# A fused layernorm, attention and expert layer on one core: stack loads in six transfers of 16 rows, statistics in four pieces, normalization on ScalarE, and the zeroed rows and first maxima at other places

## What is computed

```python
def reference(L0_attn_x, L0_attn_w_qkv, L0_attn_w_out, L0_ffn_gate_w, L0_ffn_wg, L0_ffn_wu, L0_ffn_wd):
    x = L0_attn_x
    xn = _layernorm(x, axis=-1)
    s = _L0_attn_ref(xn, L0_attn_w_qkv, L0_attn_w_out)
    g = _silu(_L0_ffn_ref(xn, L0_ffn_gate_w, L0_ffn_wg, L0_ffn_wu, L0_ffn_wd))
    x = x + s * g
    return x
```

## Time and profile before

| what | value |
|---|---|
| device time, median of 3 runs | 1719.01 us (1713.76 to 1734.11) |
| device time of the profiled execution | 1720.51 us |
| its span, first to last instruction | 1718.8 us |
| mean granted clock of TensorE, share of full | 0.965 |
| PE, DVE, ACT, POOL busy, share of the span | 91%, 81%, 68%, 10% |

### The profile page before, as it was taken

How to read it: one execution, slowest core, us unless ns; L and a number is a source line. 1 busy time by engine, 2 the same in 40 slices (tenths; PEclk the granted TensorE clock), 3 DMA queues, 4 the chain that set the end, 5 groups by cost and what they waited for, 6 DMA issues and landing times.

```text
span 1718.8 us, 29455 instructions
## 1 busy us (share of the span) xinstructions
PE 1560.9 (91%) x9121; PEld 670.6 (39%) x9121; DVE 1385.8 (81%) x1541; ACT 1174.3 (68%) x2349; POOL 169.3 (10%) x174
## 2 busy tenths in 40 slices
PE   4869799996889999999999999999999999999998
PEld 2534333333543333333333333333333333333336
DVE  6657799994348899999999999999999999999805
ACT  1332148784557777778777778777778777778771
POOL 3542222210002220000001000000010000000100
PEclk8989779998989999999999999999999999999999
DMA  3354312322432221211111122111111211111203
GB/s 133 135 181 145 124 40 71 89 77 55 140 95 64 72 69 53 80 42 41 42 41 41 40 62 68 40 40 40 40 40 40 80 50 41 40 40 40 59 4 114
DMA packets 73595, 116.51 MB, mean 68 GB/s; under 512 B 25040, under 2 KB 60240, under 8 KB 66384
## 3 DMA queue, kind: packets, MB, share of 16 engines
q1 hardware_dynamic: 65408, 101.87, 18.9%
q0 software_dynamic: 3072, 8.39, 1.6%
q10 hardware_dynamic: 5072, 5.72, 1.0%
HBM read 75.31 MB, written 39.85 MB: 67 GB/s over the span
## 4 chain that ended last, share of the span: by engine, by line
PE 71%; ACT 16%; DMA 4%; DVE 4%; issue 3%; SPq 1%; POOL 0%; ACTq 0%; DVEq 0%
PE ps L1042 29%; PE ps L1053 29%; ACT arena L548 15%; PE ps L984 3%; PE ps L1033 2%; PE ps L985 1%; PE ps L1124 1%; PE ps L1139 1%; PE ps L1007 1%; DMA x_sb<-in_x 1%; PE ps L1105 1%; PE ps L1169 1%; DMA arena<-xs_d 1%; DMA arena<-arena 1%; DVE arena L644 1%
## 5 line engine op out<-in xcount | busy, mean ns | idle before, releaser
L663 DVE TENSOR_REDUCE arena<-ps 128x1 f32<-128x1024 f32 x1000 | 1182.6, 1218 | 124.1 <-PE ps L1033 114.9
L548 ACT ACTIVATE arena<-ps 128x512 f32<-128x512 f32 x2048 | 1059.7, 603 | 269.6 <-PE ps L1042 267.8
L1033 PE MATMUL ps<-ks,qs 48*128 48x512 f32 x2000 | 803.3, 475 | 5.7 <-DVE arena L663 4.3
L1042 PE MATMUL ps<-qs,ks 50*128 50x512 f32 x2048 | 751.9, 447 | 62.1 <-ACT arena L548 30.5
L1042 PEld LDWEIGHTS ps<-qs,ks 50*128 50x128 f32 x2048 | 340.6, 185 | 683.7 <-issue 433.0
L1053 PE MATMUL ps<-arena 128*32 128x512 f32 x4096 | 548.9, 608 | 0.8 <-ACT arena L548 0.8
L1033 PEld LDWEIGHTS ps<-ks,qs 48*128 48x128 f32 x2000 | 334.6, 187 | 54.6 <-DVE arena L663 22.4
L1053 PEld LDWEIGHTS ps<-arena 128*32 128x32 f32 x4096 | 80.7, 108 | 129.3 <-ACT arena L548 112.4
L918 POOL COPY arena<-v_sb 128x256 f32 (+1 forms) x32 | 13.3, 417 | 1077.8 <-ACT arena L540 1076.2
L478 ACT COPY arena<-ps 128x512 f32<-128x512 f32 x32 | 18.8, 586 | 86.3 <-PE ps L985 86.3
L984 PE MATMUL ps<-arena 128*128 128x512 f32 x128 | 76.5, 683 | 0.7 <-ACT arena L469 0.7
(11 more groups left out here) (101 smaller groups left out, 577.5 us busy)
## 6 DMA issues: line engine op xcount, KB each, us to landing
parts_d<-arena SPq DMA_DIRECT2D x64, 256.0 KB, 2.8
qs<-parts_d SPq DMA_DIRECT2D x64, 256.0 KB
ks<-parts_d SPq DMA_DIRECT2D x64, 256.0 KB
qs<-parts_d SPq DMA_DIRECT2D x64, 128.0 KB
ks<-parts_d SPq DMA_DIRECT2D x64, 128.0 KB
xs_d<-arena SPq DMA_DIRECT2D x13, 384.0 KB, 5.3
arena<-xs_d SPq DMA_DIRECT2D x13, 384.0 KB, 3.9
ys_d<-arena SPq DMA_DIRECT2D x13, 384.0 KB, 2.8
```

What stands on the lines that cost most here:

```text
L548: nc.scalar.activation(prob[kb % 2][:, c * W:(c + 1) * W], ps[:, bank, :], ACT.Exp, scale=SCALE).then_inc(exp_done[bank], 1)
L663: nc.vector.tensor_reduce(most[head_slot][:, tile, u:u + 1], ps[:, AB + 2 * u:AB + 2 + 2 * u, :], AX.XY, ALU.max).then_inc(a_reduced[u], 1)
L1033: ins = nc.tensor.matmul(ps[:, AB + c, :], qs[head_slot][ABASE:ABASE + KR, tile * P:(tile + 1) * P].bitcast(F32R), ks[head_slot][ABASE:ABA ...
L1042: nc.tensor.matmul(ps[:, bank, :], ks[s][0:KS, kb * P:(kb + 1) * P].bitcast(F32R), qs[s][0:KS, c * W:(c + 1) * W].bitcast(F32R), start=Tru ...
```

## The change

It has six parts.

1. `stack_loads` fills each stack with three transfers of 16 rows, in all six for the two stacks, with no broadcast. The bytes are the same. `LOADS` becomes 6.
2. The statistics are taken in four pieces (tiles 0 to 3, 4 to 7, 8 to 15, 16 to 31). DVE does the last piece inside the tile loop: two tiles of `bn_stats` behind each of the tiles 0 to 7, and the short steps behind tile 7. The wait for the weights ahead of the first statistics is gone. The buffers for statistics get a place of their own.
3. The groups 1 to 7 are normalized by ACT, tile by tile, as x times the inverse deviation plus a shift (`Identity` with scale and bias). Group 1 comes before the loop, and tile t + 8 at the end of step t. DVE makes the shift with one more short step per piece. POOL keeps the rotary additions alone.
4. ACT loads the table of the square root ahead of the first one, and the table of the exponential behind the last high part, with a dummy activation on one column.
5. SP zeroes two sets of 384 rows behind each of the first seven pairs of tiles, in place of one behind each of 13, and ahead of the stack loads.
6. The maxima of tiles 12 and 13 of head 0 are computed in the last two steps of the setup, between the turns of tiles 30 and 31, and no longer behind it.

```diff
-    LOADS = 4
+    LOADS = 6
...
         def stack_loads(eng, head, qstack, kstack, base, done):
 
             rows = bass.ds(head * DH, DH)
-            eng.dma_start(qstack[base:base + 2 * DH, :],
-                          parts_d[0, 0, rows, :].unsqueeze(0).to_broadcast([2, DH, L])).then_inc(done, 16)
-            eng.dma_start(qstack[base + 2 * DH:base + 3 * DH, :], parts_d[1, 0, rows, :]).then_inc(done, 16)
-            eng.dma_start(kstack[base:base + 2 * DH, :], parts_d[:, 1, rows, :]).then_inc(done, 16)
-            eng.dma_start(kstack[base + 2 * DH:base + 3 * DH, :], parts_d[0, 1, rows, :]).then_inc(done, 16)
+            for i, (q_part, k_part) in enumerate(((0, 0), (0, 1), (1, 0))):
+                at = base + i * DH
+                eng.dma_start(qstack[at:at + DH, :], parts_d[q_part, 0, rows, :]).then_inc(done, 16)
+                eng.dma_start(kstack[at:at + DH, :], parts_d[k_part, 1, rows, :]).then_inc(done, 16)
...
+                for i in range(2 * p, min(2 * p + 2, NF // ZR)):
+                    clear_rows(i)
                 if p == NT // 4 - 1:
...
-                if p < NF // ZR:
-                    clear_rows(p)
...
+            def normal(t):
+
+                if t % GT == 0:
+                    act.wait_ge(norm_ready, max(k for k in range(len(XCUT) - 1) if XCUT[k] <= t) + 1)
+                ins = nc.scalar.activation(gate[:, t, :], x_sb[:, t, :], ACT.Identity, bias=shift_x[:, t:t + 1],
+                                           scale=rstd[:, t:t + 1])
+                if t % GT == GT - 1:
+                    ins.then_inc(xn_ready, 1)
...
+            act.wait_ge(first_ones, 1)
+            nc.scalar.activation(table_in[32:64, 0:1], ks[0][32:64, 0:1], ACT.Sqrt, scale=0.0)
+            root(0)
...
-            act.wait_ge(var_ready, 2)
-            nc.scalar.activation(tmp[:, 3, GT:NT], tmp[:, 2, GT:NT], ACT.Sqrt).then_inc(std_ready, 1)
+            root(1)
+            for t in range(GT, 2 * GT):
+                normal(t)
+            root(2)
             for t in range(NT):
...
                     high_part(t - LAG)
+                if t + 2 * GT < NT:
+                    normal(t + 2 * GT)
+                if t == 2 * GT - 1:
+                    root(3)
             for t in range(NT - LAG, NT):
                 high_part(t)
+            nc.scalar.activation(table_in[32:64, 1:2], ks[0][32:64, 0:1], ACT.Exp, scale=0.0)
...
-            dve.wait_ge(first_loaded, 16 * 2)
-            moments(0, (0,))
...
-            moments(1, (1, 2, 3))
+            for k in range(2):
+                dve.wait_ge(x_loaded[k], 16)
+                statistics(XCUT[k], XCUT[k + 1])
+                moments(k)
+                inverse(k)
...
-            for t in range(NT - LAG, NT):
-                low_part(t)
+                if t < 2 * GT:
+                    statistics(XCUT[3] + 2 * t, XCUT[3] + 2 * t + 2)
+                if t == 2 * GT - 1:
+                    moments(3)
+                    inverse(3)
+                    assert count[0] == SETUP_STEPS
+            for t in range(NT, NT + LAG):
+                reduce_early(t - EARLY, 0)
+                low_part(t - LAG)
+                reduce_early(t - EARLY, 1)
...
-            normal(1)
-            normal(2)
             for t in range(NT):
                 add_turned(t)
-                n, j = divmod(t, GT)
-                if j == 2 and n + 3 < NG:
-                    normal(n + 3)
...
-            for t in range(NT - LAG, NT):
-                turn_q(t)
+            for t in range(NT, NT + LAG):
+                score_early(t - EARLY, 0)
+                turn_q(t - LAG)
+                score_early(t - EARLY, 1)
```

More of the change, by code:

```diff
@@ L201, in layer_kernel @@
         std_ready = sem("std_ready")
[L202 removed]
+        norm_ready = sem("norm_ready")
         xn_ready = sem("xn_ready")
@@ L581, in link, with statistics, moments @@
                     dve.wait_ge(dve_step, base[0] + count[0])
-            def moments(k, pieces):
-                ts = slice(XCUT[pieces[0]], XCUT[pieces[-1] + 1])
-                for i in pieces:
-                    dve.wait_ge(x_loaded[i], 16)
-                    for t in range(XCUT[i], XCUT[i + 1]):
-                        nc.vector.bn_stats(stats[:, t, :], x_sb[:, t, :]).then_inc(stats_done, 1)
+            def statistics(lo, hi):
+                for t in range(lo, hi):
+                    nc.vector.bn_stats(stats[:, t, :], x_sb[:, t, :]).then_inc(stats_done, 1)
+            def moments(k):
+                ts = slice(XCUT[k], XCUT[k + 1])
                 dve.wait_ge(stats_done, ts.stop)
@@ L605, in _ @@
                 nc.vector.memset(ks[i][32:64, :], -1.0).then_inc(first_ones, 1)
-            dve.wait_ge(first_loaded, 16 * 2)
-            moments(0, (0,))
-            for j in range(GT):
-                ins = nc.vector.tensor_scalar(gate[:, j, :], x_sb[:, j, :], mean[:, j:j + 1], rstd[:, j:j + 1],
-                                              ALU.subtract, ALU.mult)
-            ins.then_inc(xn_ready, 1)
-            moments(1, (1, 2, 3))
+            for k in range(2):
[3 more added lines that the diff above has]
+                inverse(k)
+                if k == 0:
+                    for j in range(GT):
+                        ins = nc.vector.tensor_scalar(gate[:, j, :], x_sb[:, j, :], mean[:, j:j + 1], rstd[:, j:j + 1],
+                                                      ALU.subtract, ALU.mult)
+                    ins.then_inc(xn_ready, 1)
+            dve.wait_ge(x_loaded[2], 16)
+            statistics(XCUT[2], XCUT[3])
+            moments(2)
+            inverse(2)
+            dve.wait_ge(x_loaded[3], 16)
             dve.wait_ge(weights_loaded, 16 * NW)
@@ L644, in reduce_early @@
                 nc.vector.tensor_reduce(most[0][:, t, u:u + 1], ps[:, 6:8, :], AX.XY, ALU.max).then_inc(a_reduced[u], 1)
-            assert count[0] == SETUP_STEPS
             for t in range(NT):
@@ L726, in _ @@
             choose()
-            for t in range(NT - EARLY, KB):
+            for t in range(NT + LAG - EARLY, KB):
                 for u in range(2):
@@ L1059, in _ @@
             pe.wait_ge(qkv_out, NT)
-            for t in range(NT - EARLY, AHEAD):
+            for t in range(NT + LAG - EARLY, AHEAD):
                 if t == KB:
```

25 lines of the change are left out of this document (11 added, 14 removed).

## The result

The changed kernel takes 1674.54 us (median of 4 runs, 1672.07 to 1677.56) against 1716.77 us before (4 runs). The ratio is 0.9757, with a 95% interval of 0.9726 to 0.9789: faster, by 42 us. The forecast was 1665.1. Some of the 48.5 is chance: it is 6 us more than the medians give.

What follows compares the result with a forecast made beforehand. PE was taken to bound the heads (134.97 of 140 us busy), so only its waits could be won: 17.3 + 11.5 + 10.6 + 10.7 + 1.6 + 2.4 + 1.3 = 55.4 off 1720.51 gave 1665.1 us, range 1652 to 1688.

Steps and rivals of the forecast that it cites:

- Start and tiles 5 to 20: Setup: PE's 9.69 us wait for group 1 goes, 17.3 us gained to tile 5; undisturbed groups then gain 11.5.
- The rival of a setup bound by its chain: Setup: late ACT copies hold DVE and PE's turns, 4.0 us a tile for 3.3, 14 us less gain, 1679; chance 0.15.
- The first stack load: PE's 13.10 us wait at the first early score: six 16-row transfers land by 118.3, gain 10.6, bounds 5 and 13.
- Two of the signs named for a right forecast: First early score near 89 us after a 2 to 3 us wait; sorted rows landing within 5 us of issue.
- Ports: Stack loads: 16 rows in 16 partitions run at half rate, 2 us more at each of two waited loads, 1669; chance 0.12.
- The experts: PE's 12.09 us wait at the experts' first sorted rows: they land at 404.5, gain 10.7, bounds 5 and 12.1.
- The reciprocal's wait: DVE's 1.59 us wait at 556 for a small transfer behind a stack load goes: 1.6, bounds 0 and 2.5.
- The slower rival: Heads: six transfers fill all engines ahead of the small transfer of sums; DVE waits in 31 heads, 49 us; chance 0.02.
- End of the setup: Two tiles of maxima leave the run behind the loop, 5.1 us; the loop ends 2.7 later; net 2.4, bounds 0 and 5.
- The table's term: First exponential: the exponential's table load of 1.28 us that stood ahead of it is hidden; gain 1.3 us.
- What the clock gives back after shorter waits is not counted: Whole kernel: any gain from PE's granted clock after shorter waits was left out of the sum of 55.4 us.
- forecast as summed: Device time of the whole kernel with the terms as added up, 1655 to 1676 us; chance 0.60.

Runs made afterwards that it cites:

- e4: Changed kernel with groups 1 to 7 normalized by POOL again, the four pieces of statistics kept: 1688.37 us.
- m1: Transfers of 8 KB rows alone on an idle core, x copied unchanged, each set twice; six of 16 rows as in the kernel took 8.5 us.
- e1: Changed kernel with the four old stack transfers put back: 1688.81 us.
- e5: Changed kernel with the zeroing of 384 rows back behind each of the first 13 pairs of tiles: 1669.33 us.
- e3: Changed kernel with the maxima of tiles 12 and 13 computed behind the setup loop again: 1672.87 us.
- e10: Changed kernel with each block's rows on every fourth partition in the maxima's stacks (free rows zeroed once by POOL), every third in the others: 1673.13 us.
- e6: Changed kernel without the two table loads ahead of their use: 1673.14 us.
- e9: Changed kernel with each block's rows on every third partition and the zeroing back behind each of 13 pairs of tiles: 1674.67 us.

## Why the prediction was right and where it failed

**Start and tiles 5 to 20** came out as worked: 17.3 and 11.5 forecast, 17.3 and 11.7 measured, tile 5 at 33.00 and groups at 13.30 us. The cause, POOL's pass over DVE's product, was there again in e4 (2.07 for 0.69). That the wait of 9.69 us was the late statistics' shows in e4 as well, where it stays away. Four normalizations on ACT took 2.08 us, 0.52 each, where 0.384 had been taken from another activation; with 2 us in hand it didn't matter. The rival of a setup bound by its chain did not come; its only trace is the wait of 0.88 us that had been charged with 1.5.

**The first stack load** is where the sum failed first. The step was "So the transfers of 16 rows (128 KB) take 0.35 us on all engines": the bursts of the earlier trace rows were each a transfer with none of its kind ahead of it. From "by 115.9, and the last lands 2.5 us later" came a load of 4.8 us, bound by its issues. It took 8.5, bound by 1.14 us for each queued transfer, and the term of 10.6 measured 7.2. It was inside its bounds of 5 to 13. Two of the signs named for a right forecast failed with it: the first early score came at 92.72 after a wait of 5.90, not near 89 after 2 to 3, and the sorted rows 6.9 us after their issue, not within 5. The rival named Ports had the mechanism; it had a chance of 0.12, because I took the burst in the earlier trace rows for a rate. Its price from those bursts, 2 us a load, was still too low: 3.6 us. That the old 32-row transfers were the slow ones, at one or two tenths busy, was right (12.7 us for two alone in m1, and the waits in e1).

**The experts.** The term of 10.7 measured 9.3: PE's wait fell from 12.09 to 3.96, which is 8.1, and the rest of the stretch gave 1.2. That rest isn't told from chance: with waits of 4.0, 4.1 and 3.9 us the stretch from the fourth to the fifth reciprocal took 131.3 us in the changed kernel, 132.6 in e5 and 134.0 in e3. The step that failed is the same, "behind 2 us of wide transfers". e10 takes the wait down to 1.8.

**The reciprocal's wait** of 1.59 us in one head went, and with what lay behind it 2.5 was won for 1.6. The slower rival, a wait at each head, has no row: in the heads between the experts and the last ones the DMA ends no wait of the reciprocal.

**End of the setup.** The term of 2.4 came at 1.8, but not by its mechanism, so this near hit is luck. The step that failed was "so the loop ends some 2.7 us later": the stretch grew by 4.4 us against before (16.00 for 11.55) and by 4.8 against e3, and of the 5.1 us that leave the run behind the loop 0.6 and 0.2 remain. The other part of the 1.8 is one step at half clock fewer than before (1.7 us), less 0.5 for the step behind the first early score. The table's term of 1.3 holds: without the dummy activation the way from head 0 to the first exponential is 1.3 us longer in e6 (2.19 for 0.91). Neither shows in the time. "What the clock gives back after shorter waits is not counted" left out a place where it takes: 3.0 us in the first head.

The terms that came short, 3.4, 1.4, 0.6 and 3.0, less 1.5 that came over, are the 6.9 us between 55.4 and 48.5. By the medians 42 us were won; the execution profiled before was 3.7 us above its median, and the one after 2.2 below. The time fell into the stretch of "forecast as summed", 1655 to 1676, near its slow end. The price of the rival Ports, 1669, lies in the same stretch and nearer, so the time alone doesn't tell which of the two rates held; the rows do.

## What to carry to other kernels

Take the rate of a queued transfer from a row that has several of them in a queue: one burst shows what a lone transfer does (2.7 us, nearly all latency) and hides a limit that nearly doubled the load. Where the rows of an operand may stand in any order, spread those of one transfer over the partitions: every fourth in place of adjacent ones took six transfers from 8.4 to 5.8 us, and PE's wait in the kernel from 5.9 to 3.2. Look where the free rows are zeroed: on POOL at the start it cost DVE and PE 2.3 us. And don't expect a saving of a few us to show in the time when a stretch at half clock follows it; look at the rows at its end instead. Before a difference between two places is put down to an edit, cut it where the edit begins: 2.1 of the 2.3 us between e3 and the changed kernel lay ahead of it.

## What was not expected of the hardware

The granted clock in the last head fell for 65 us in the profiled execution of e10. Three of its six executions were 22 us longer, with the same low mean clock (0.964), more than the transfers brought. The kernel before shows the like in its time: beside 1712.74 to 1720.54 us with a mean clock of 0.963 to 0.969 stand single executions at 1734.99 to 1737.5 with 0.947 to 0.95, e1 has one at 1711.63 with 0.953, and e9 one at 1690.82 with 0.960, beside 0.973 to 0.979. They were not profiled, so that they have the same cause is only likely.

A transfer recorded as busy need not move bytes. The same 786 KB took 0.70 of 8.45 us on adjacent partitions and 0.42 of 5.83 on every fourth, and the share of q1 in the kernel went from 18.9% to 31.8%, 25.7% and 22.9% at the same 101.9 MB, with no relation to whether the load was quicker than before.

The Trainium skill (DMA: Bandwidth & Descriptors, Why a DMA increments its semaphore by 16 and not by 1) has a transfer use as many engines as divide the slowest dimension, two for a source of [2, 16, ...]. m1 agrees: 41 GB/s at 0.10 of the engines' time, in a run with nothing beside it.
